# Attention stage: one PSUM bank moved from the row ring to the column ring, and the mixing matmuls of a set spread over four steps

## What is computed

```
x = x + _L0_conv_ref(_gn(x), ...)
# inside, for each of 2 entries x 8 channels and each of 8 heads:
qk = jnp.einsum('bceqd,bcekd->bceqk', q, k) / math.sqrt(h)      # 512 x 512
a = jax.nn.softmax(qk, axis=-1)
o = jnp.einsum('bceqk,bcekd->bceqd', a, v)
# then a 256 x 256 projection of each channel, and a mix of the channels
x = x + _L1_conv_ref(_gn(x), weight, bias)
```

## Time and profile before

| | us |
|---|---|
| median of 3 runs | 1254.8 (1251.63 to 1258.26) |
| the profiled execution, own time | 1258.79 |
| its span, first to last instruction | 1256.9 |
| PE busy in the span | 1079.0 (86%) |
| DVE busy | 933.5 (74%) |
| POOL busy | 871.2 (69%) |
| ACT busy | 663.2 (53%) |
| attention, first row scores to last mixing round | about 412.7 to 974.1 |

### The profile page before, as it was taken

How to read it: one execution, slowest core, us unless ns; L and a number is a source line. 1 busy time by engine, 2 the same in 40 slices (tenths; PEclk the granted TensorE clock), 3 DMA queues, 4 the chain that set the end, 5 groups by cost and what they waited for, 6 DMA issues and landing times. The chain is left out here.

```text
span 1256.9 us, 26231 instructions
## 1 busy us (share of the span) xinstructions
PE 1079.0 (86%) x10648; PEld 590.9 (47%) x10648; DVE 933.5 (74%) x1225; ACT 663.2 (53%) x1110; POOL 871.2 (69%) x812
## 2 busy tenths in 40 slices
PE   0299999999894699899998999999988589899998
PEld 0177777777673123333333333333333345355553
DVE  3789999999764798788888888888872584544344
ACT  1555555555442066666666666666666223346345
POOL 0467776777583489899998899988999007937900
PEclk9899999999998589999999999999999799899999
DMA  9725244332644555527171736254000599875661
GB/s 305 238 83 161 76 124 116 104 94 67 139 105 99 115 77 126 111 55 116 49 121 35 122 65 114 57 94 81 31 19 18 184 354 299 265 228 155 190 214 54
DMA packets 137759, 159.02 MB, mean 127 GB/s; under 512 B 17852, under 2 KB 85708, under 8 KB 137640
## 3 DMA queue, kind: packets, MB, share of 16 engines
q1 hardware_dynamic: 113448, 119.37, 39.6%
q10 hardware_dynamic: 15648, 28.81, 6.6%
q0 software_dynamic: 8544, 9.18, 2.8%
HBM read 106.48 MB, written 52.89 MB: 127 GB/s over the span
## 5 line engine op out<-in xcount | busy, mean ns | idle before, releaser
L1108 POOL TENSOR_TENSOR a_pl<-a_prob 128x512 bf16<-128x512 f32 x416 | 443.1, 1094 | 37.0 <-ACT a_prob L1059 36.4
L1012 DVE TENSOR_REDUCE a_negmax<-a_row 128x1 f32<-128x512 f32 x512 | 334.1, 706 | 60.4 <-PE a_row L939 59.2
L1059 ACT ACTIVATE a_prob<-a_col 128x512 f32<-128x512 f32 x512 | 292.1, 596 | 147.0 <-PE a_col L960 140.7
L710 POOL TENSOR_TENSOR f_yl<-f_y,f_yh 128x768 bf16<-128x768 f32 x80 | 132.8, 1679 | 95.8 <-ACT f_yh L657 95.8
L657 ACT ACTIVATE f_yh<-f_y 128x768 bf16<-128x768 f32 x80 | 67.4, 844 | 139.1 <-DVE f_y L548 121.2
L1023 DVE TENSOR_TENSOR a_pl<-a_prob 128x512 bf16<-128x512 f32 x96 | 123.3, 1285 | 19.2 <-ACT a_prob L1059 19.2
L450 PE MATMUL f_acc<-f_wh,f_xh 128*32 128x384 bf16 x1280 | 110.9, 335 | 29.8 <-DVE f_wl L538 26.5
L939 PE MATMUL a_row<-k,q 96*128 96x512 bf16 x256 | 106.6, 423 | 22.7 <-PEq L202 14.9
L960 PE MATMUL a_col<-a_q,a_k 98*128 98x512 bf16 x256 | 97.9, 388 | 23.2 <-ACT a_prob L1059 19.3
L960 PE MATMUL a_col<-q,k 98*128 98x512 bf16 x256 | 99.8, 390 | 16.1 <-ACT a_prob L1059 14.7
L714 POOL TENSOR_TENSOR f_straight<-f_straight,f_turned 128x832 f32<-128x832 f32 x40 | 107.0, 2675 | 9.4 <-DVE f_turned L565 9.4
(11 more groups left out here) (156 smaller groups left out, 2189.2 us busy)
## 6 DMA issues: line engine op xcount, KB each, us to landing
X<-b_x ACTq DMA_DIRECT2D x16, 526.0 KB, 8.3
q<-in_x SPq DMA_DIRECT2D x8, 1024.0 KB, 7.7
a_v<-V SPq DMA_DIRECT2D x16, 512.0 KB, 4.4
Z<-a_z ACTq DMA_DIRECT2D x32, 256.0 KB, 3.5
b_z<-Z SPq DMA_DIRECT2D x16, 512.0 KB, 11.0
b_x<-in_x SPq DMA_DIRECT2D x32, 256.0 KB, 10.1
b_res<-X SPq DMA_DIRECT2D x38, 208.0 KB
out<-b_y ACTq DMA_DIRECT2D x38, 208.0 KB
```

The lines of the kernel that those rows point to most:

```text
L710: nc.gpsimd.tensor_tensor(yl[half][n % 2][:], y[half][:], yh[half][n % 2][:], ALU.subtract).then_inc(yl_done, 1)
L1012: nc.vector.reduce_max(negmax[n % PAIR][:, 0, t:t + 1], row[step % ROWS][:], AX.X, negate=True).then_inc(max_done, 1)
L1059: nc.scalar.activation(prob[sets_done % RING][:, t % QUAD, :], col[step % 2][:], ACT.Exp).then_inc(exp_done, 1)
L1108: nc.gpsimd.tensor_tensor(pl[p][:, r, :], prob[p][:, r, :], ph[p][:, r, :], ALU.subtract).then_inc(lo_pool, 1)
```

## The change

The row ring gets 2 banks, the column ring 3. The rounds of a set are no longer issued together: `ROUNDS` gives for each of the four slots of a set the rounds that are issued there. For kt = 0 these are none, 0 and 1, 2, 3 and 4; for kt = 1 and 2 they are 0, 1, 2, 3 and 4; for kt = 3 they are 0 to 2, 3 and 4, none, none. The logarithm waits for a semaphore of its own, set after round 1 of the fourth set, where it waited for round 4. The division is one slot later, and so is everything from the tail on (slots 22 to 25 and 27 to 30). The number of instructions of each kind stays what it was.

```diff
-        ROWS = 3
+        ROWS, COLS = 2, 3
...
-        col = [ps(f"a_col{s}", [P, W]) for s in range(2)]
+        col = [ps(f"a_col{s}", [P, W]) for s in range(COLS)]
...
-        TAIL = KEEP + QUAD * QT + 2
+        TAIL = KEEP + QUAD * QT + 3
+        ROUNDS = [((), (0, 1), (2,), (3, 4))] + [((0,), (1,), (2,), (3, 4))] * (QT - 2) + [((0, 1, 2), (3, 4), (), ())]
...
-        def sets(first, emit):
-            return [(STEPS * n + first + QUAD * g, lambda n=n, g=g: emit(n, g)) for n in range(UNITS) for g in range(SETS)]
+        def rounds(first, emit):
+            return [(STEPS * n + first + QUAD * g + t, lambda n=n, g=g, j=j: emit(n, g, j))
+                    for n in range(UNITS) for g in range(SETS) for t in range(QUAD) for j in ROUNDS[g % QT][t]]
...
-                if step >= 2:
-                    pe.wait_ge(exp_done, step - 1)
+                if step >= COLS:
+                    pe.wait_ge(exp_done, step - COLS + 1)
...
-            def mix_set(n, g):
+            def mix_round(n, g, j):
...
+                if j == 0:
+                    pe.wait_ge(lo_pool, pool_lows(n, g))
+                    pe.wait_ge(lo_dve, dve_lows(n, g))
...
+                if j == 2:
...
+                    if kt == 0 and quad:
+                        pe.wait_ge(divided, quad)
+                part = (ph, pl, ph, ph, pl)[j]
+                for r in range(QUAD):
+                    h = g // QT * QUAD + r
+                    to, weights = (weight, ones[:]) if j < 2 else (mix, (vl if j == 3 else vh)[n % 2][:, kt, h * DH:(h + 1) * DH])
+                    last = nc.tensor.matmul(to[r * DH:(r + 1) * DH, :], weights, part[p][:, r, :],
+                                            start=kt == 0 and j in (0, 2), stop=kt == QT - 1 and j in (1, 4))
+                if j == 1 and kt == QT - 1:
+                    last.then_inc(weighed, 1)
+                if j == 4:
+                    last.then_inc(mixed, 1)
...
-            pipeline(steps(0, row_max) + units(SPLIT, split_max) + lows(EXP + 1, low_part, False) + quads(KEEP, divide))
+            pipeline(steps(0, row_max) + units(SPLIT, split_max) + lows(EXP + 1, low_part, False) + quads(KEEP + 1, divide))
...
-                act.wait_ge(mixed, QT * (quad + 1))
+                act.wait_ge(weighed, quad + 1)
```

More of the change, by code:

```diff
@@ L798, in attend @@
         mixed = sem("a_mixed")
+        weighed = sem("a_weighed")
         logged = sem("a_logged")
@@ L957, in col_scores @@
                     pe.wait_ge(max_in[n % PAIR], 16 * (n // PAIR + 1))
-                if step >= 2:
-                    pe.wait_ge(exp_done, step - 1)
-                nc.tensor.matmul(col[step % 2][:].rearrange("p (t w) -> p t w", t=QT), k[s][:, h, kt, m, :], q[s][:, h, :, m, :],
+                if step >= COLS:
+                    pe.wait_ge(exp_done, step - COLS + 1)
+                nc.tensor.matmul(col[step % COLS][:].rearrange("p (t w) -> p t w", t=QT), k[s][:, h, kt, m, :], q[s][:, h, :, m, :],
@@ new lines, in mix_round @@
+                if j == 0:
+                    pe.wait_ge(lo_pool, pool_lows(n, g))
+                    pe.wait_ge(lo_dve, dve_lows(n, g))
+                    if n == g == 0:
+                        pe.wait_ge(ones_set, 1)
+                    if kt == 0 and quad:
+                        pe.wait_ge(logged, quad)
+                if j == 2:
+                    if g == 0:
+                        pe.wait_ge(v_lo, n + 1)
+                    if kt == 0 and quad:
+                        pe.wait_ge(divided, quad)
@@ L999, in tail @@
                     last.then_inc(out_full, 1)
-            pipeline(units(TURN, turn_max) + steps(EXP, col_scores) + steps(0, row_scores) + sets(MIX, mix_set) + tail_parts(TAIL, tail))
+            pipeline(units(TURN, turn_max) + steps(EXP, col_scores) + steps(0, row_scores) + rounds(MIX, mix_round) + tail_parts(TAIL, tail))
         @block.vector
@@ L1058, in exp @@
                 act.wait_ge(col_full, step + 1)
-                nc.scalar.activation(prob[sets_done % RING][:, t % QUAD, :], col[step % 2][:], ACT.Exp).then_inc(exp_done, 1)
+                nc.scalar.activation(prob[sets_done % RING][:, t % QUAD, :], col[step % COLS][:], ACT.Exp).then_inc(exp_done, 1)
             def log_weight(n, m):
                 quad = SETS // QT * n + m
-                act.wait_ge(mixed, QT * (quad + 1))
+                act.wait_ge(weighed, quad + 1)
                 nc.scalar.activation(logs[quad % 2][:], weight[:], ACT.Ln).then_inc(logged, 1)
```

## The result

The changed kernel takes 1333.3 us in the median (1329.4 to 1348.4, 4 runs), the kernel before 1253.5 in the same comparison: a ratio of 1.065 (95% interval 1.056 to 1.074). It is slower by 80 us. Forecast were +45 us and a range up to 1317. The direction came out as forecast and the waits stand in most of the places named, but the size is outside the range. The steps that failed are PE's work in a unit (31.6 us forecast, 33.0 measured, in part because a tail part behind rounds is dearer), the clock taken as full after the start (11.5 us), and the cost of the start (14 us and not 4).

The account below looks back on a forecast made before the run. The small rings between nearly full PE, DVE and POOL were taken as the bound: 14.3 periods x (36.2 - 33.2) = +43, start +4, end -2, so +45 on 1254.8: 1300 us, range 1266 to 1317.

Parts of the forecast that it names:

- the clock taken as full after the start: Half clock was priced only for the first units; later units were priced with no loss from a lower clock.
- the cost of the start: First units with row scores alone: two row banks cost 0.10 us more on some 38 slots, +4 us.
- The waits of PE: PE waiting at slots 1, 6, 7, 18, 22 and 23 with two row banks: 4.6 us a unit.
- Crossings: On PE, 36 more switches between full and quarter arrays a unit, 0.09 us each: +3.2 us, work 28.4 to 31.6.
- the low price: On DVE, the low part of slot 8 taken at 0.6 us, as with POOL idle; the other five at 1.4.
- The end: After the last row scores POOL is less behind and the last logarithm is earlier: -2 us.
- The third column bank: Lets ACT fall two slots behind, so PE's waits for ACT, 2.4 us a unit, were put at nothing.
- The earlier logarithm: On ACT, about 0.7 us off the wait of each quad; counted as nothing inside a unit.
- PE's work as the bound: Row ring forgiving, waits under 1.6 us a unit: unit takes PE's 31.6 us, 1234 us in all; chance 0.12.
- Lone rounds: Single rounds on PE switch arrays for free: work stays 28.4 us, unit about 33.9, 1267 us; chance 0.12.
- DVE's low parts: Mostly 0.6 us because POOL has free time, halving row waits: 33.9 us a unit, near 1267; chance 0.14.
- Rival 4: PE's waits for ACT return despite three column banks: up to 2.4 us a unit, 1317 with half; chance 0.10.

Follow-up runs that it names:

- e2: The changed kernel with three row banks and two column banks, its spread rounds, early logarithm, later division and later tail kept: 1299.4 us, ratio 1.035.
- e1: The kernel before with only the banks changed, to two row banks and three column banks: 1322.9 us, ratio 1.054.
- e4: The changed kernel with useless matmuls added where PE stands: 5 and 3 in slots 6 and 7, 7 before the division's wait: 1328.3 us, ratio 1.059.
- e6: The changed kernel with useless matmuls added where PE stands: 4 and 2 in slots 6 and 7, 6 before the division's wait: 1325.4 us, ratio 1.058.
- e8: e3 with two row banks and three column banks and nothing else changed: 1303.6 us, ratio 1.040.
- e3: The changed kernel with three row and two column banks, rounds regrouped into 12 groups a unit, division in its old slot: 1236.4 us, ratio 0.986.
- e7: The kernel before with only the logarithm's wait changed, to round 1 of the fourth set instead of round 4: 1251.6 us, ratio 0.996.
- e9: e3 with the third set of a quad one slot later, the fourth in groups of 3 and 2 rounds, the tail one slot later: 1230.1 us, ratio 0.982.

## Why the prediction was right in direction and too small

- **The waits of PE: the size right, the cause right in part.** 4.6 us of waits a unit were walked, 4.4 are there, 3.9 of them in the slots named: 1.15 and 0.75 for the walked 1.2 and 0.8 (slots 6 and 7), 0.29 for 0.3 and 1.73 for 1.7 (slots 22 and 23). The walked waits of slots 1 and 18 did not come, and slot 11 has 0.46, because the low part of slot 8 took 1.6 us and not the cheap 0.6. All of it was filed under the second row bank, but the largest, the 1.73, is the wait for the division. In the waits view it is 1.6 here, was 0.7 before, and is 1.3 in e2 with three row banks, so most of its growth does not come from the bank. The division's later slot is the likely source, but e1, with the old slot and two row banks, has 1.1 as well, and no run moves the division alone. What the bank adds to the rest of the change is 1.3 us a period, and e2's period of 36.1 was already the 36.2 forecast for everything. That 4.6 came so near to 4.4 is in part luck: slots 1 and 18 too much, slot 11 too little.
- **Crossings: the price was right and a term beside it was missing.** Row scores to a round is 0.31 again, and 36 more crossings cost 3.2. But PE's work in a period is 37.4 - 4.4 = 33.0 us and not 31.6. The step that failed is "a tail part is 0.44": that is one behind scores. Behind a round it takes 0.55 (818.46 to 819.01), which before held for two parts of eight and now for seven. A lone round and its way back cost 0.02 more than a round in a group, 14 times. That and the tail parts' 0.6 us are 0.9; the other 0.5 is spread over many small distances and not accounted for. On DVE the split of slot 0 took 0.82 us and not 0.18:

```profile
784.01 0.82 DVE L1021 TENSOR_TENSOR a_negmax<-a_negmax 128x32 f32<-128x32 f32 x1
```

  Sized right, the periods are worth 14.3 x 4.2 = +60 and not +43: 17 of the missing 35 us.
- **A price misread.** The low part at 807.81 was read as one beside an idle POOL. But POOL began its next operation at 807.97, so it shows only that POOL stood when this one began. The walk then gave slot 8 the low price. In the changed kernel that low part began at 792.63, while POOL's `v_low` ran (2.13 us from 791.57), and took 1.6 us.
- **The clock: the term that the sum did not have.** The prediction used the half clock for the start alone and took 1.00 after it, while it forecast itself that PE would stand 1 to 2 us at three places of each unit. The trace shows 11.5 us in single periods, and e4 and e6 show the cause.
- **The start: +14 instead of +4.** 4.0 came as forecast in the 32 slots of row scores alone (30.4 instead of 26.5 us to the first turn), 3.8 for the first 29 slots behind slot 54, and 6 are left, while the clock stood at 0.84 (before: 1.00):

```profile
450.00:487.00 37.00, 32.46 (x194) 7.10 (x193) 29.91 (x42) 21.65 (x37) 30.73 (x29) 0.84 0.43 70
```

  That the clock made these 6 is likely and not shown, since the fillers gave back only 0.7 (e4) and 2.2 (e6) of them. The ring's part is shown: the same stretch takes 80.8 us in e1 against 70.7 before, 84.8 after against 72.8 in e2, and 79.4 in e8 against 69.2 in e3. In these three pairs two row banks cost 10 to 12 us there.
- **The end:** +4 instead of -2. The two stages that the change does not touch took 8 us less, which hides part of the loss.
- **The third column bank: right.** The 2.0 us a period that PE's matmuls waited for exponentials are gone from the list of waits. The bank was hardly needed for it: in e2, with two column banks, 0.6 us was left, and in e3 0.2.
- **The earlier logarithm: right** that it is nearly nothing, 0.2 us a unit (e7).
- **The rivals.** PE's work as the bound did not come. Lone rounds do not cross for nothing. DVE's low parts did not get cheap, although POOL had 7.5 us free in a period: 1.4 to 1.6 in five of six, 1.0 in the sixth. Rival 4's 1317 was the nearest, with a wrong mechanism. I had bounded the top of the range by ACT's waits coming back, where a fall of the clock and a dearer tail part were the open ends.
- **The estimate by the Trainium skill** ("TensorE: Matmul & The Clock Gate", Single matmul latency, about 166 ns warm, at each crossing) would have given 34.4 us of PE work. Measured were 33.0, and the single crossing is still at 0.09. On what the prediction left out, the Trainium skill says on the same page, in Part 1, that the clock gate lowers TensorE's clock when the engine has been idle. The trace agrees in the direction: the matmuls went from 0.38 to 0.61 us, here behind single waits of 1.6 us and less.

## What to carry to other kernels

Between two engines that are both nearly full, compare each ring with the longest block that stands on its consumer (here 2.0 us of low part and division against two banks of 0.6 us each), and walk the slots in order before moving a bank. The third row bank was worth 3.6 us a period in one order of the rounds and 1.3 in another, so price it in the order that it will have. Rounds in another array mode did well in few groups (e3, e9) and badly when spread (e2): each group costs 0.18 us of crossings, and an fp32 part behind it 0.11 more. When two parts of a change can each make a wait, look at what the waiting instruction names: the longest wait here named the division, not the ring. And a forecast that puts waits on PE has to price the clock too: here 11.5 of 80 us in the periods, and perhaps 6 more at the start.

## What was unexpected of the hardware

- The clock's price under waits: the same unit took 37.4 us at 1.00, 39.0 at 0.96, 40.4 at 0.92 and 43.1 at 0.84. Useless matmuls in the waits brought 43.1 down to 38.1. No single wait of PE in these periods was longer than 1.6 us, and equal waits brought a fall in five of thirteen periods.
- An fp32 tail part costs 0.55 us behind rounds of the 32-column array and 0.44 behind full-array matmuls.
- A tiny DVE operation of 128x32 took 0.18 us in most units of the kernel before and 0.82 in most units after, with POOL at work beside it in both. At 800.18 before it began where one of POOL's operations ends (three in 3.08 us from 799.18), and at 784.01 after in the middle of one (three in 3.12 from 782.66), and it ended about when that one did. These are two places; no run varied it.
